# A decoder layer on one core: evacuation of the side banks, and the splitting of q and k, moved further behind TensorE

## The reference

```python
x = layernorm(x + self_attention(x))           # logits get log(penalty), computed from a gate sigmoid(x @ Wg)
x = layernorm(x + cross_attention(x, ctx))     # logits get mask * -1e9; output goes through Wo
x = layernorm(x + ffn(x))                      # activations and weights fake-quantised to 8 bits
# attention: softmax(q k^T / 4 + bias) v, q = x Wq + bq, k = src Wk + bk, v = src Wv + bv, in float32
```

## Time and profile before

| what | value |
|---|---|
| median of 3 runs | 867.48 us (865.65 to 867.61) |
| profiled execution, its own time | 860.73 us |
| its span | 858.9 us |
| TensorE busy | 685.7 us, 80% |
| VectorE busy | 611.4 us, 71% |
| ScalarE busy | 478.6 us, 56% |
| GpSimd busy | 327.6 us, 38% |

### The profile page before, as it was taken

The page is one execution under the profiler, slowest core; times in us unless marked ns, Lnnn a source line. Parts: engine busy times, 40 slices in busy tenths (PEclk is TensorE's granted clock), DMA queues, the critical chain, the costliest instruction groups (busy, mean ns, idle before and its releaser), DMA issues.

```text
span 858.9 us, 10704 instructions
## 1 busy us (share of the span) xinstructions
PE 685.7 (80%) x3348; PEld 264.3 (31%) x3350; DVE 611.4 (71%) x1576; ACT 478.6 (56%) x800; POOL 327.6 (38%) x417
## 2 busy tenths in 40 slices
PE   6077788998788799998887998987787899856662
PEld 3052223343222243443222433422222233223231
DVE  3978684675698766668967666697975577527996
ACT  3213456555455868744558686454366576944634
POOL 6103655655466404454663143563513001001314
PEclk9587899999999999999999999997899899996966
DMA  3533033120322314221223132331112220000002
GB/s 98 151 119 94 22 95 95 58 65 19 83 69 65 89 30 130 62 49 45 67 69 90 34 102 60 94 96 42 40 40 73 77 72 10 3 1 0 2 0 98
DMA packets 34887, 53.85 MB, mean 63 GB/s; under 512 B 4368, under 2 KB 25872, under 8 KB 34832
## 3 DMA queue, kind: packets, MB, share of 16 engines
q1 hardware_dynamic: 32912, 51.61, 20.9%
q10 hardware_dynamic: 1920, 1.57, 1.2%
HBM read 36.91 MB, written 14.68 MB: 60 GB/s over the span
## 4 chain that ended last, share of the span: by engine, by line
PE 44%; DVE 26%; POOL 11%; ACT 8%; issue 7%; DMA 3%; SPq 1%; ACTq 0%; POOLq 0%; DVEq 0%
PE ps L1446 10%; PE ps L1402 9%; DVE unused L931 8%; POOL probs L652 7%; PE ps L1422 6%; PE ps L1389 6%; PE ps L1305 5%; ACT probs L836 4%; PE ps L1382 2%; PE ps L1427 2%; PE ps L1426 2%; DMA KS<-parts_kc 2%; POOL rest L678 1%; DVE x L968 1%; DVE stats L953 1%
## 5 line engine op out<-in xcount | busy, mean ns | idle before, releaser
L1402 PE MATMUL ps<-KS,QS 96*128 96x512 bf16 x512 | 203.6, 399 | 83.5 <-DVE mx L931 55.6
L652 POOL TENSOR_TENSOR probs<-probs,penT 128x512 f32<-128x512 f32 x128 | 166.7, 1321 | 161.0 <-ACT probs L836 161.0
L836 ACT ACTIVATE probs<-ps 128x512 f32<-128x512 f32 x256 | 146.6, 597 | 142.6 <-PE ps L1427 103.0
L931 DVE CUSTOM_DVE_ANT_0 unused<-ps,lp 128x512 bf16<-128x512 f32 x256 | 169.9, 686 | 73.8 <-PE ps L1402 69.5
L1422 PE MATMUL ps<-QS,KS 108*128 108x512 bf16 x512 | 198.8, 393 | 12.6 <-ACT probs L836 12.6
L836 ACT ACTIVATE probs<-ps,mask_col 128x512 f32<-128x512 f32 x256 | 165.1, 688 | 55.3 <-PE ps L1422 53.7
L931 DVE CUSTOM_DVE_ANT_0 unused<-ps,mask_rest 128x512 bf16<-128x512 f32 x192 | 127.2, 685 | 49.1 <-PE ps L1402 48.8
L1402 PEld LDWEIGHTS ps<-KS,QS 96*128 96x128 bf16 x512 | 50.6, 99 | 265.6 <-DVE mx L931 183.9
L1446 PE MATMUL ps<-probs,v_s 128*32 128x512 f32 x512 | 72.4, 638 | 11.3 <-POOL probs L652 10.5
L1446 PE MATMUL ps<-probs,v_c 128*32 128x512 f32 x512 | 69.9, 619 | 0.9 <-ACT probs L836 0.9
L1422 PEld LDWEIGHTS ps<-QS,KS 108*128 108x128 bf16 x512 | 50.4, 100 | 59.9 <-ACT probs L836 30.2
(11 more groups left out here) (186 smaller groups left out, 941.9 us busy)
## 6 DMA issues: line engine op xcount, KB each, us to landing
parts_qs<-parts SPq DMA_DIRECT2D x8, 384.0 KB, 2.6
parts_ks<-parts SPq DMA_DIRECT2D x8, 384.0 KB, 3.1
QS<-parts_qs SPq DMA_DIRECT2D x16, 192.0 KB
KS<-parts_ks SPq DMA_DIRECT2D x16, 192.0 KB
parts_kc<-parts SPq DMA_DIRECT2D x8, 384.0 KB, 2.6
parts_qc<-parts SPq DMA_DIRECT2D x8, 384.0 KB, 2.9
QS<-parts_qc SPq DMA_DIRECT2D x16, 192.0 KB
KS<-parts_kc SPq DMA_DIRECT2D x16, 192.0 KB
```

Source lines behind the costliest of these rows:

```text
L652: g.tensor_tensor(probs[:, T % NP, :], probs[:, T % NP, :], penT[:, MUL_KT.index(kt), :], ALU.mult)\
L836: s_.activation(probs[:, T % NP, :], ps[:, EXP_BANKS[T % 3], :], ACT.Exp, bias=bias)\
L931: v.tensor_tensor_reduce(out=unused[:, i % 2, :], in0=ps[:, MAX_BANKS[i % 2], :], in1=lp[:, t, :] if kind == "s" else mask_row(b), scale=1 ...
L1402: mm(ps[:, MAX_BANKS[i % 2], :], QS[0:SK, slot, j, t * P:(t + 1) * P], KS[0:SK, slot, j, :], start=True, stop=True).then_inc(max_scores, 1)
```

## The change

Four things change. VectorE does norm, v, wo and lpB three slots behind TensorE (two before); its other side work stays at two. ScalarE makes the middle part three slots behind the slot of its q or k. GpSimd makes the low part five slots behind it. The plan now places only the q and k jobs themselves, puts "middle" and "low" in the same slot as their projection, and keeps the two halves of a task at least four slots apart. Where several lags meet in a slot, the job from the earliest slot comes first.

```diff
--- before.py
+++ after.py
@@ -45,6 +45,9 @@
 MUL_KT = (0, 2)
 
 DVE_LAG, ACT_LAG, POOL_LAG = 2, 0, 1
+DVE_LATE = {"norm": 3, "v": 3, "wo": 3, "lpB": 3}
+ACT_LATE = {"middle": 3}
+POOL_LATE = {"low": 5}
 NP = 8
 QMAX = 127.0
 MAGIC = 12582912.0
@@ -73,7 +76,7 @@
     what, rest = task[0], task[1:]
     if what in ("q", "k"):
         jobs = [(what, *rest, c) for c in range(HC)]
-        return [j for job in jobs for j in (job, ("middle", *job), ("low", *job))]
+        return jobs
     if what == "v":
         return [(what, *rest, i) for i in range(NT // 2)]
     if what == "gate":
@@ -101,6 +104,7 @@
 
 
 
+QK_APART = 4
 QUIET_SLOTS = (0, 1, 4, 5, 8, 9, 12, 13)
 LONG_SLOTS = (1, 5, 9, 13)
 
@@ -141,8 +145,10 @@
                     near = [i for i in (LONG_SLOTS if long_job(job) else QUIET_SLOTS)
                             if slot <= i <= slot + 1 and not any(j[0] in BANK_JOBS for j in s.items[i])]
                     slot = near[0] if near else slot
-                    after = min(slot + 1, TG - 1)
+                    after = min(slot + (QK_APART if job[0] in ("q", "k") else 1), TG - 1)
                 s.items[slot].append(job)
+                if job[0] in ("q", "k"):
+                    s.items[slot] += [("middle", *job), ("low", *job)]
 
         for slot in range(1, TG):
             if any(job[0] in BANK_JOBS for job in s.items[slot - 1]):
@@ -434,13 +440,18 @@
 
         slots = [(s, i) for s in steps for i in range(TG)]
 
-        def slots_behind(lag):
-
-
-            for k in range(len(slots) + lag):
+        def slots_behind(lag, late):
+
+
+            lags = sorted({lag, *late.values()}, reverse=True)
+            for k in range(len(slots) + lags[0]):
                 s, i = slots[k] if k < len(slots) else (None, None)
-                before_s, before_i = slots[k - lag] if k >= lag else (None, None)
-                yield s, i, before_s.items[before_i] if before_s else []
+                jobs = []
+                for behind in lags:
+                    if 0 <= k - behind < len(slots):
+                        then, at = slots[k - behind]
+                        jobs += [job for job in then.items[at] if late.get(job[0], lag) == behind]
+                yield s, i, jobs
 
         def units_of(t):
             return [unit[job] for job in expand(t) if job in unit]
@@ -694,7 +705,7 @@
 
             for job in PROLOGUE:
                 do(job)
-            for s, i, items in slots_behind(POOL_LAG):
+            for s, i, items in slots_behind(POOL_LAG, POOL_LATE):
                 if s is not None and s.p2 is not None and groups[s.p2][0] == "s" and i // GH in MUL_KT:
                     multiply(s.p2, i)
                 for job in items:
@@ -839,7 +850,7 @@
             act.wait_ge(gate_ready, 1)
             for job in PROLOGUE:
                 do(job)
-            for s, i, items in slots_behind(ACT_LAG):
+            for s, i, items in slots_behind(ACT_LAG, ACT_LATE):
                 if s is not None and s.p2 is not None:
                     exponential(s.p2, i)
                 for job in items:
@@ -1161,7 +1172,7 @@
             for job in PROLOGUE:
                 do(job)
             v.memset(amax[:, :], 0.0)
-            for s, i, items in slots_behind(DVE_LAG):
+            for s, i, items in slots_behind(DVE_LAG, DVE_LATE):
                 if s is not None and s.p1 is not None:
                     row_max(s.p1, i)
                 for job in items:
```

## The result

| kernel | median | range, runs |
|---|---|---|
| before | 865.40 us | 861.22 to 869.83, 8 |
| with the change | 872.99 us | 869.48 to 875.21, 8 |

The ratio is 1.0078, with a 95% interval of 1.0043 to 1.0113: the change makes the kernel slower, by 7.6 us in the medians. The prediction said 1.0077. Timed once more later (experiment 9), the ratio was 1.0064 (1.0043 to 1.0084). So the sum came out. Its terms did so less well: A and B were each a little too small, and D and E were each off by several us.

The account below looks back on a forecast made before the run. TensorE's queue was taken to set the pace in most places. 4.0 + 3.7 + 9.5 - 4.9 - 5.7 = +6.6 us (0.77%) gave 874.1 us on the 867.48 us median; range 869 to 880, 8 in 10 for 864 to 882.

Parts of the forecast that it names:

- A: Step 7: the second low part ends later, so the stack lands later and TensorE waits longer; +4.0 us.
- B: Step 27: the second middle and low parts come later, so the stack lands later and TensorE waits; +3.7 us.
- D: Steps 2, 4, 9, 17: exponentials go ahead of the middle part, saving four GpSimd waits of 1.23 us; -4.9 us.
- E: Eleven places, steps 0, 5, 13, 14, 21, 31: row maxima go ahead of VectorE's side work; -5.7 us.
- C: Twelve places: VectorE gives banks back a row maximum later, so TensorE starts later; +9.5 us (10.7 read).
- The rival that late banks cost nothing: VectorE's later hand-back falls on existing TensorE waits, so C is 0; sum -2.9 us, 864.6 us; chance 0.15.
- The rival that the stacks come no later: Low parts come as early as before, so no A or B; sum -1.1 us, 866.4 us; chance 0.15.
- the clock a rival: Step 2: the shortened TensorE wait could keep the clock up; sum +4.1 us, 871.6 us; chance 0.08.
- theory 2: Forecast for experiment 9: late banks meet stretches the splitting tightened; the change at least 4 us over its parts' sum.

Follow-up runs that it names:

- experiment 9: The change once more, unchanged, timed beside its two parts: 871.20 us, 1.0064 of the kernel before.
- 2: The change with all of VectorE's side work back at two slots, so the splitting's lateness alone: 863.22 us, 0.9972 of the kernel before.
- 11: Same kernel as 2, timed again (the change with VectorE as before): 863.75 us, 0.9964 of the kernel before.
- 12: The kernel before with only norm three slots behind in VectorE's queue: 875.49 us, 1.0108 of the kernel before.
- 3: The change with norm alone back at two slots behind; v, wo and lpB stay at three: 862.97 us, 0.9967 of the kernel before.
- 10: Same kernel as 1, timed again (the kernel before with VectorE's norm, v, wo, lpB three slots behind): 868.73 us, 1.0028.
- 1: The kernel before with only VectorE's norm, v, wo and lpB three slots behind: 868.57 us, 1.0047 of the kernel before.
- experiment 8: The kernel before with SP storing the first q half, loading the stack, then storing the second in steps 7 and 27: 862.00 us, 0.9965.
- experiment 5: The change with SP storing the first q half, loading the stack, then storing the second in steps 7 and 27: 858.11 us, 0.9921.
- 4: The change with the q halves of steps 7 and 27 at their old lags and distance: 865.55 us, 1.0000 of the kernel before.

## Why the prediction was right in sum, and where its steps were wrong

| term | predicted | measured | from |
|---|---|---|---|
| A, stack of step 7 | +4.0 | +4.4 to +4.9 | step 7 in 2, 11, 9 and the change |
| B, stack of step 27 | +3.7 | +4.3 to +4.5 alone, +5.1 to +6.1 in the change | step 27 in 2, 11; 9 and the change |
| C, late banks | +9.5 | +9.4 for norm alone; +8.4 to +9.6 in the change | 12; 9 and the change against 3 |
| D, ScalarE and GpSimd no longer stop | -4.9 | -9 to -11 | seven steps in 2 and 11; -11.4 by their medians less A and B |
| E, row maxima go first | -5.7 | -6.8 alone, -0.25 by the medians in the change, both with v's late places in them | 12 and 10; 2 and 3 |
| sum | +6.6 | +5.1 to +7.6 | 9 and the change |

**C** was right in place and mechanism, and its size came out. In the twelve places read at 10.7 us the waits are 9.5 us; the other 1.3 of the 10.8 us stand in steps 7 and 27, which the prediction had put into A and B. Step 10 was read at 0.95 and is 0.89, the v places of steps 11 and 19 at 1.0 and are 0.74. The 9.5 us of the sum was 10.7 less a part that would run into idle time. What was less was the waits themselves, so that figure is met in part by luck. The rival that late banks cost nothing is out: 12 alone rules it out.

**A** and **B** were right in mechanism and 0.5 to 0.9 us too small each, with VectorE's part of the change away. The stack waits are 15.0 and 16.4 us, where about 16 was forecast. The rival that the stacks come no later is out too. In B the middle part now stands behind three exponentials of ScalarE, and GpSimd is idle for 1.33 us between rest and low part (1.29 on the chain, 0.74 in before). In the change the norm in front of the second q half is late as well.

**D** was the mis-sized term. I priced four waits of 1.23 us. The steps named (2, 4, 9, 17) gave 0.7 to 2.7, 1.0 to 1.1, 1.7 and 1.5 to 1.7, and steps 6, 13 and 26, which I had not named, gave 4.0 more. The figure for step 2 is everything up to the norm of step 3, and it isn't safe to give it to D: experiments 1 and 10, without the splitting, are 1.6 and 1.4 us early there as well. The count of such waits was short as well: the earlier trace rows calls that of step 17 the last of five, but the kernel before has two more, at 84.27 and 589.35 us.

In step 13 no wait is shorter at all. Windows of before and of experiment 11, from the same place of the step to the next norm (busy us of TensorE, its weight loads, VectorE, ScalarE and GpSimd, then the granted clock, the DMA share and GB/s):

```profile
355.00:360.82 5.82, 5.82 (x30) 2.32 (x30) 3.96 (x16) 2.79 (x6) 5.03 (x9) 0.71 0.41 106
```

```profile
355.00:358.85 3.85, 3.85 (x26) 1.89 (x25) 3.05 (x12) 2.57 (x5) 3.55 (x7) 1.00 0.42 98
```

In front of these windows TensorE runs the same instructions with the same two waits (1.04 and 0.38 us in before, 1.03 and 0.38 in 11). Then, in before, the same product takes twice as long, and in 11 it does not:

```profile
357.18 1.94 PE L1446 MATMUL ps<-probs,v_c 128*32 128x512 f32 x8
```

```profile
356.54 1.06 PE L1457 MATMUL ps<-probs,v_c 128*32 128x512 f32 x8
```

One fall of the clock was there and is not there any more, and it is worth 1.6 us. It isn't one execution's chance: step 13 is as long in experiment 8, whose program is the one of before there, and 1.6 us shorter in both 2 and 11. Step 9 is like it: before's clock falls there too, at 271 us, and in 2 and 11 it does not. So a good part of what D gave is not the waits that I counted but falls of the clock that no longer happened. Why the clock stayed up in step 13 after the same two waits, the rows don't say; it stays open.

What the prediction said would show for D was also half wrong. ScalarE's idle time before middle parts fell from 37.1 to 19.3 us, not under 12. ScalarE and TensorE in step 2, to be read beside the earlier trace rows:

```profile
88.99 0.63 ACT L766 ACTIVATE parts<-rest 128x512 bf16<-128x512 f32 x1 [2.77 <-POOL rest L689]
...
90.78 1.07 PE L1457 MATMUL ps<-probs,v_s 128*32 128x512 f32 x8 [2.83 <-POOL probs L663]
```

The waits of 1.23 us for exponentials are gone from steps 2, 4, 9 and 17, as forecast, but three slots are not enough where GpSimd is busy: the rest still comes 2.77 us after ScalarE is ready for it, and TensorE waits 2.83 us for the multiplication. The clock there did stay up this time (94 to 97 us):

```profile
94.00:97.00 3.00, 2.86 (x17) 0.76 (x15) 2.82 (x6) 3.00 (x7) 1.86 (x2) 1.00 0.03 9
```

In experiment 3, whose program is the same up to there, TensorE waited 2.69 us and the same window has 0.59; in the kernel before it has 0.50. The Trainium skill, "TensorE: Matmul & The Clock Gate", section "Why this matters for your kernels", which made the clock a rival, speaks of long idle gaps. The trace agrees that the clock falls behind such a gap in the kernel before; here an idle time of the same length was followed by a full clock, so the gap alone does not decide. Five profiles are of one program up to the norm of step 3: the change is at -4.07 us there, experiment 5 at -4.21, 3 and 4 at -1.72 and -1.65, and the change's second profile (experiment 9) at +0.56. Single profiles differ by that much from chance alone.

**E** was about right in the kernel before (6.8 us for 5.7) and too large in the kernel for which I used it. Experiment 12 against 10 shows where it lay: steps 5, 13, 17 and 21 (0.9, 3.0, 1.6, 1.3). With the splitting late too, step 17's wait and half of step 13's gain are there already, and they can't be had twice: 3 against 11 still gains 0.9, 1.4, 0 and 1.3 in those steps, 3.7 in all. Against it stands v late, which costs 1.9 us in step 30 (3 against 2) and its waits in steps 11 and 19. By the medians of experiments 2 and 3, 0.25 us is left, uncertain by about 3 us; from step 3 on, the profile of 3 is 3.9 us ahead of that of 2 and 2.9 ahead of that of 11. So E is smaller in the change than alone, but how small isn't shown.

**The terms don't add.** By the medians the change is 4.8 us over the sum of its halves. One place is clear. In step 13 each half gains (-2.17 and -1.59 us) and both together only -2.17, in all four profiles that have both halves there (the change, 9, 4 and 5): the same fall of the clock can be saved only once. That is 1.6 us.

Step 10 looks like a second place, and is not shown to be one. The halves cost 0.83 and 0.57 us there, and together 2.85 and 2.94 in the two profiles of the change. TensorE in the change, behind the late k half:

```profile
288.27 0.39 PE L1413 MATMUL ps<-KS,QS 96*128 96x512 bf16 x1 [0.67 <-DVE mx L942]
...
289.22 0.39 PE L1413 MATMUL ps<-KS,QS 96*128 96x512 bf16 x1 [0.34 <-DVE mx L942]
...
290.25 0.38 PE L1413 MATMUL ps<-KS,QS 96*128 96x512 bf16 x1 [0.43 <-DVE mx L942]
...
290.78 1.94 PE L1457 MATMUL ps<-probs,v_c 128*32 128x512 f32 x8
```

```profile
290.70:294.00 3.30, 3.30 (x13) 0.64 (x12) 2.33 (x9) 0.97 (x2) 0.00 (x0) 0.51 0.00 0
```

Three waits under 0.7 us stand within 3 us, and then the clock is at its lower level (0.51) for 3.3 us. But experiment 5 has both halves in step 10 too, with the same late k half (0.88 us) and the same three waits, and there the clock stays up:

```profile
280.07 0.39 PE L1415 MATMUL ps<-KS,QS 96*128 96x512 bf16 x1 [0.67 <-DVE mx L944]
...
281.02 0.39 PE L1415 MATMUL ps<-KS,QS 96*128 96x512 bf16 x1 [0.34 <-DVE mx L944]
...
282.05 0.38 PE L1415 MATMUL ps<-KS,QS 96*128 96x512 bf16 x1 [0.43 <-DVE mx L944]
...
282.58 1.07 PE L1459 MATMUL ps<-probs,v_c 128*32 128x512 f32 x8
```

Experiment 4 is like it. In these two, step 10 costs 1.39 and 1.40 us, which is the sum of the halves. Experiments 3 and 11 have the three waits without the late k half, and a clock that stays up. So the fall stands in two of four profiles with both halves. That can be chance, or something further back that 4 and 5 don't share; theory 2's reason, that the clock falls because late banks meet tighter stretches, is neither shown nor ruled out here.

The rest isn't placed. Other steps go the other way (in step 30 both together cost 1.5 to 1.6 us less than the sum of the halves, in step 25 2.2 to 3.0 less), and over all steps the profiled executions of the change are between 0.8 us under and 1.9 us over the sum of the profiled halves. Those compare single executions with that one profile of before, so the excess rests on the medians alone.

So +6.6 was met because D gave 4 to 6 us more than forecast, while E gave less in the change than alone, and A and B took more. Those errors ran against each other, and that they came so near to cancelling is luck. The account isn't closed either: the measured terms of the table add up to anything between 6 and 11 us, for a measured sum of 5.1 to 7.6.

## What to carry to other kernels

With two banks in turn, whoever empties a bank sets when the next unit but one may start: before work on an engine is put a slot later, look at every place where that unit starts at once, and put off only the jobs whose bank has room (here norm had none, and one entry cost 9.4 us). A transfer that is needed in the same step should wait only for the part that it reads: storing the first half, loading, then storing the second was worth 12.4 to 13.6 us here, once the halves were apart. When an edit has two halves, run each alone before trusting a sum, since two halves can save the same wait or the same fall of the clock only once (step 13). And before a fall of the clock is given to an edit, look at the same place in every profile that shares the program there.

## What the runs showed of the hardware

The same waits were followed by either level of the clock. In step 10, behind one wait of 0.88 or 0.89 us and then three of 0.67 or 0.68, 0.34 and 0.43 us, the clock fell in two executions (the change and experiment 9; granted clock 0.51 for 3.3 and 3.5 us, the product of eight matmuls took 1.94 us) and stayed up in two others (experiments 4 and 5; 1.06 and 1.07 us). In step 7 the clock was 0.58 behind a wait of 2.56 us in the change, and 1.00 behind one of 2.55 us in experiment 5. Behind three waits of 0.52, 0.54 and 0.61 us in step 9 of experiment 11 it stayed up too. So these rows don't give the condition. A fall in step 10 or 13 cost 1.5 to 1.6 us, a little more than the 1.4 us of short waits right ahead of it. The same program differed by up to 4.8 us up to step 3 from one execution to the next (-4.21 and +0.56).
